# The first stage's transpose of normalized x: TensorE, or memory and VectorE

## The reference, cut to what matters

```python
mod = (_silu(L0_c) @ L0_wmod).reshape(L0_c.shape[0], 6, 1, -1)
sa, ca, ga, sb, cb, gb = (mod[:, n] for n in range(6))
ga = (2 * (ga >= 0) - 1) * jnp.maximum(jnp.abs(ga), 0.25)     # gb alike
h = _layernorm(x) * (1 + ca) + sa
x = x + ga * attention(h, wq, wk, wv, wo)          # 32 query heads, 8 key/value heads of 32
h = _layernorm(x) * (1 + cb) + sb
x = x + gb * experts(h, router, A, B)              # top 2 of 4 low-rank experts
```

## Time and profile before

| | us |
|---|---|
| median of 3 runs | 2801.24 (2797.73 to 2801.27) |
| the profiled execution | 2795.91 |
| its span | 2794.1 |
| PE busy | 2752.4 |
| DVE busy | 2181.9 |
| ACT busy | 1529.4 |
| POOL busy | 1909.4 |

### The profile page before, as it was taken

How to read it: one execution, slowest core, us unless ns; L and a number is a source line. 1 busy time by engine, 2 the same in 40 slices (tenths; PEclk the granted TensorE clock), 3 DMA queues, 4 the chain that set the end, 5 groups by cost and what they waited for, 6 DMA issues and landing times.

```text
span 2794.1 us, 48987 instructions
## 1 busy us (share of the span) xinstructions
PE 2752.4 (99%) x14654; PEld 1695.8 (61%) x14654; DVE 2181.9 (78%) x2809; ACT 1529.4 (55%) x2959; POOL 1909.4 (68%) x710
## 2 busy tenths in 40 slices
PE   7999999999999999999999999999999999999998
PEld 4788888884444444444444444444444447888887
DVE  4433434348999999999999999999999968676667
ACT  3211111116777676777767777767777764455454
POOL 2433333317999999999999999999999996111110
PEclk9999999999999999999999999999999999999999
DMA  7544443434444334334334334344444443323332
GB/s 268 181 144 137 147 139 132 137 116 137 91 88 100 87 87 100 85 87 100 85 87 100 85 89 98 89 90 93 93 90 91 97 123 114 113 96 108 113 100 81
DMA packets 167645, 307.05 MB, mean 110 GB/s; under 512 B 50001, under 2 KB 91409, under 8 KB 159505
## 3 DMA queue, kind: packets, MB, share of 16 engines
q1 hardware_dynamic: 158496, 240.05, 29.5%
q0 software_dynamic: 9072, 66.06, 11.6%
HBM read 159.12 MB, written 79.82 MB: 86 GB/s over the span
## 4 chain that ended last, share of the span: by engine, by line
PE 74%; DVE 2%; ACT 0%; issue 0%; DVEq 0%; POOL 0%; ACTq 0%; POOLq 0%
PE back_ps L1348 22%; PE back_ps L1362 18%; PE s_ps L1322 17%; PE s_ps L1938 11%; PE back_ps L1379 2%; PE back_ps L1987 2%; PE back_ps L2006 1%; PE back_ps L1959 1%; DVE mx L1237 1%; PE back_ps L1337 0%; PE s_ps L1411 0%; DVE a_lo L1281 0%; ACT h_t L1719 0%; DVE two_sum L1252 0%; DVE xn L1793 0%
## 5 line engine op out<-in xcount | busy, mean ns | idle before, releaser
L1218 ACT ACTIVATE p_t<-back_ps 128x512 f32<-128x512 f32 x2048 | 1114.7, 596 | 432.5 <-PE back_ps L1348 390.7
L1237 DVE TENSOR_REDUCE mx<-s_ps 128x1 f32<-128x1024 f32 x1002 | 1172.4, 1208 | 83.9 <-PE s_ps L1322 76.2
L1128 POOL TENSOR_TENSOR p_sum<-p_sum,p_t 128x2048 f32<-128x2048 f32 x254 | 1166.2, 4591 | 24.8 <-ACT p_t L1218 7.9
L1348 PE MATMUL back_ps<-q_st,k_st 98*128 98x512 f32 x2048 | 809.9, 436 | 3.4 <-POOL ones L1097 2.4
L1348 PEld LDWEIGHTS back_ps<-q_st,k_st 98*128 98x128 f32 x2048 | 343.9, 187 | 592.1 <-ACT p_t L1218 495.7
L1322 PE MATMUL s_ps<-k_st,q_st 96*128 96x512 f32 x2004 | 633.0, 397 | 0.6 <-DVE mx L1237 0.3
L1362 PE MATMUL back_ps<-p_t,v_sb 128*32 128x512 f32 x4096 | 545.8, 605 | 0.0
L1322 PEld LDWEIGHTS s_ps<-k_st,q_st 96*128 96x128 f32 x2004 | 379.0, 189 | 72.5 <-DVE mx L1237 3.2
L574 POOL TENSOR_TENSOR o_lo<-side,o_hi 128x512 fp32r<-128x512 f32 x80 | 104.2, 1303 | 321.4 <-ACT o_hi L544 321.2
L1252 DVE TENSOR_REDUCE two_sum<-p_t 128x512 f32<-128x1024 f32 x256 | 317.8, 1243 | 2.1 <-ACT p_t L1218 2.1
L1128 POOL TENSOR_TENSOR p_sum<-p_t 128x2048 f32<-128x2048 f32 x64 | 312.9, 4889 | 8.6 <-ACT p_t L1218 8.6
(11 more groups left out here) (186 smaller groups left out, 2910.8 us busy)
## 6 DMA issues: line engine op xcount, KB each, us to landing
p_sum<-two_sum POOLq DMA_DIRECT2D x63, 1024.0 KB, 6.9
q_st<-q_hi_d SPq DMA_DIRECT2D x128, 256.0 KB, 4.3
stage<-w_mod SPq DMA_DIRECT2D x48, 512.0 KB, 6.4
q_hi_d<-o_hi SPq DMA_DIRECT2D x64, 256.0 KB, 2.0
q_lo_d<-o_lo SPq DMA_DIRECT2D x64, 256.0 KB, 2.0
...
att_d<-a_sb SPq DMA_DIRECT2D x128, 128.0 KB, 2.3
...
```

Of the source, the lines that this page charges most:

```text
L1128: nc.gpsimd.tensor_tensor(total, before, p_t[:, kt, :, :], ALU.add).then_inc(sum_done, 1)
L1218: nc.scalar.activation(p_t[:, s, c, :], st_ps[:, c % 2, :], ACT.Exp, scale=SCALE)\
L1237: nc.vector.tensor_reduce(mx[:, slot % 2, e:e + 1], s_ps[:, e % 2, :], AX_X, ALU.max)\
L1348: nc.tensor.matmul(st_ps[:, c % 2, :], k_st[:, slot // 2, s * P:(s + 1) * P], q_st[:, slot, jj, h * QW:(h + 1) * QW], start=True, stop=True)\
```

## The change

In blocks 1 to 7 the normalized x of a half is no longer turned by PE. "away" stores the half to a new internal tensor `xn_d` (1 MB, one DMA, rows of 4 KB). "back" loads it with four DMAs, one for each quarter of the partitions, in runs of 32 numbers (128 bytes), into `squares`, which is the space of slots 2 and 3 of `stage`: for each tile of 128 features the squares of 32 x 32 then lie where a transpose within the square completes the whole transpose. DVE does that, one instruction of 128 x 256 a tile, into the same PSUM tile as before, and its scale-and-shift follows with a wait for it. Block 0's own h still goes through PE. "rows" has two slots left, so it comes in four parts of two slots where it came in two parts of four. The tables of events move stats, norm and turn of both halves.

```diff
...
@@ -215,23 +218,27 @@
 
 
 
-    PREPARE = {-1: [("fetch", 0)], 0: [("stats", 0)], 1: [("norm", 0)], 2: [("turn", 0, 0), ("turn", 0, 1)],
-               3: [("turn", 0, 2), ("turn", 0, 3)], 4: [("turn", 0, 4), ("turn", 0, 5)],
-               5: [("turn", 0, 6), ("turn", 0, 7), ("fetch", 1)], 7: [("stats", 1)], 8: [("norm", 1)],
-               9: [("turn", 1, 0), ("turn", 1, 1)], 10: [("turn", 1, 2), ("turn", 1, 3)],
+
+    PREPARE = {-1: [("fetch", 0)], 0: [("stats", 0), ("norm", 0)], 1: [("away", 0)], 2: [("back", 0), ("fetch", 1)],
+               4: [("stats", 1), ("norm", 1), ("turn", 0, 0), ("turn", 0, 1), ("turn", 0, 2)],
+               5: [("turn", 0, 3), ("turn", 0, 4), ("turn", 0, 5), ("away", 1)], 6: [("turn", 0, 6), ("turn", 0, 7)],
+               7: [("back", 1)], 9: [("turn", 1, 0), ("turn", 1, 1)], 10: [("turn", 1, 2), ("turn", 1, 3)],
                11: [("turn", 1, 4), ("turn", 1, 5)], 12: [("turn", 1, 6), ("turn", 1, 7)]}
 
-    MODULATE = {-1: [("rows", 0)], 3: [("mod", 0), ("rows", 1)], 11: [("mod", 1)]}
-
-
-    PREPARE_FIRST = {-1: [("fetch", 0)], 3: [("stats", 0)], 4: [("norm", 0)],
-                     5: [("turn", 0, 0), ("turn", 0, 1), ("turn", 0, 2)],
-                     6: [("turn", 0, 3), ("turn", 0, 4), ("turn", 0, 5)],
-                     7: [("turn", 0, 6), ("turn", 0, 7), ("fetch", 1)], 8: [("stats", 1)], 9: [("norm", 1)],
-                     10: [("turn", 1, 0), ("turn", 1, 1), ("turn", 1, 2)],
-                     11: [("turn", 1, 3), ("turn", 1, 4), ("turn", 1, 5)],
-                     12: [("turn", 1, 6), ("turn", 1, 7)]}
-    MODULATE_FIRST = {6: [("rows", 0)], 8: [("mod", 0), ("rows", 1)], 11: [("mod", 1)]}
+    MODULATE = {-1: [("rows", 0)], 2: [("mod", 0), ("rows", 1)], 5: [("mod", 1), ("rows", 2)],
+                8: [("mod", 2), ("rows", 3)], 11: [("mod", 3)]}
+
+
+    PREPARE_FIRST = {-1: [("fetch", 0)], 2: [("stats", 0), ("norm", 0)], 3: [("away", 0)], 4: [("fetch", 1)],
+                     5: [("back", 0)],
+                     6: [("stats", 1), ("norm", 1)], 7: [("turn", 0, 0), ("turn", 0, 1), ("turn", 0, 2), ("away", 1)],
+                     8: [("turn", 0, 3), ("turn", 0, 4), ("turn", 0, 5), ("turn", 0, 6), ("turn", 0, 7)],
+                     9: [("back", 1)],
+                     11: [("turn", 1, 0), ("turn", 1, 1), ("turn", 1, 2)],
+                     12: [("turn", 1, 3), ("turn", 1, 4), ("turn", 1, 5)],
+                     13: [("turn", 1, 6), ("turn", 1, 7)]}
+    MODULATE_FIRST = {5: [("rows", 0)], 7: [("mod", 0), ("rows", 1)], 9: [("mod", 1), ("rows", 2)],
+                      11: [("mod", 2), ("rows", 3)], 13: [("mod", 3)]}
 
 
     BESIDE_LAST = {-1: [("pairs",)], 12: [("negate",)], 13: [("scores", AHEAD - 2), ("scores", AHEAD - 1)]}
...
@@ -314,6 +321,7 @@
         h_lo = (sb("h_lo0", [P, KT, BLK], F32R), sb("h_lo1", [P, KT, BLK], F32R))
         stage = at("stage", [P, SLOTS, D], F32, q_at)
         xn = at("xn", [P, HT, D], F32, q_at + SLOTS * D * 4)
+        squares = stage[:, MOD_SLOTS:SLOTS, :].rearrange("p s (k n) -> p (s k) n", n=HALF)
         h_f = sb("h_f", [P, 2, HALF], F32)
         side = sb("side", [P, 3 * BLK + 4 * HALF], F32)
         o_hi = at("o_hi", [P, 2, BLK], F32R, q_at + (SLOTS + HT) * D * 4)
...
@@ -383,10 +394,30 @@
             def _(sp):
                 def fetch(half):
 
-                    if not is_int(half, 0):
-                        sp.wait_ge(turned, half * KT)
+                    if is_int(half, 2):
+                        sp.wait_ge(turned, 2 * KT)
+                    elif not is_int(half, 0):
+                        sp.wait_ge(xn_out, half * 16 - 32)
                     sp.dma_start(xn[:, :, :], x[bass.ds(half * HALF, HALF), :].rearrange("(t p) d -> p t d", p=P))\
                       .then_inc(x_in, 16)
+
+                def put_away(half):
+                    sp.wait_ge(xn_ready, half + 1)
+                    sp.dma_start(xn_d[bass.ds(half * HALF, HALF), :].rearrange("(t p) d -> p t d", p=P), xn[:, :, :])\
+                      .then_inc(xn_out, 16)
+
+                def bring_back(half):
+
+
+
+                    if is_int(half, 2):
+                        sp.wait_ge(wkv_lo_done, KT)
+                    for n in range(4):
+                        src = xn_d[bass.ds(half * HALF, HALF), :].rearrange("(b t) (k n c) -> n t k b c", t=32, n=4, c=32)[n]
+                        dst = squares[32 * n:32 * n + 32, :, :].rearrange("t k (b c) -> t k b c", c=32)
+                        if n == 0:
+                            sp.wait_ge(xn_out, half * 16 - 16)
+                        sp.dma_start(dst, src).then_inc(squares_in, 16)
 
                 sp.dma_start(cs[:, :, :], c_t).then_inc(small_in, 16)
                 sp.dma_start(ident[:, :], ident_in).then_inc(small_in, 16)
...
@@ -481,12 +516,12 @@
 
                                 sp.wait_ge(wkv_lo_done, KT)
 
-                            sp.wait_ge(stage_used, vec * (2 * SLOTS) + (MOD_CHUNKS + ev[1] * SLOTS))
-                            for s in range(SLOTS):
+                            sp.wait_ge(stage_used, vec * KT + (MOD_CHUNKS + ev[1] * MOD_SLOTS))
+                            for s in range(MOD_SLOTS):
                                 sp.dma_start(stage[:, s, :],
-                                             w_mod_t[:, ev[1] * SLOTS + s, bass.ds(vec * D + 2 * D, D)])\
+                                             w_mod_t[:, ev[1] * MOD_SLOTS + s, bass.ds(vec * D + 2 * D, D)])\
                                   .then_inc(stage_in[s], 16)
-                        elif ev == ("mod", 1):
+                        elif ev == ("mod", MOD_PARTS - 1):
                             sp.wait_ge(row_ready, vec + 1)
                             for j in range(4):
                                 src = slice(32 * j, 32 * j + 25, 8)
...
@@ -645,13 +680,20 @@
                             hf, kt = ev[1:]
                             tile = tile_at(i, hf, kt)
                             bank = bank_at(i, hf, kt)
-                            dve.wait_ge(turned, tile + 1)
+                            source = t_ps[:, bank, 0:HALF]
+                            if is_int(i, -1):
+                                dve.wait_ge(turned, tile + 1)
+                            else:
+                                if kt == 0:
+                                    dve.wait_ge(squares_in, i * 128 + 64 * hf + 64)
+                                nc.vector.transpose(source, squares[:, kt, :]).then_inc(x_turned_done, 1)
+                                dve.wait_ge(x_turned_done, tile - 2 * KT + 1)
                             if not (is_int(i, -1) and kt == 0):
 
                                 dve.wait_ge(h_lo_done, tile - 1)
 
                             at = b + par
-                            nc.vector.tensor_scalar(h_f[:, bank, :], t_ps[:, bank, 0:HALF],
+                            nc.vector.tensor_scalar(h_f[:, bank, :], source,
                                                     scale1[:, kt, bass.ds(at, 1)], shift[:, kt, bass.ds(at, 1)],
                                                     ALU.mult, ALU.add).then_inc(h_ready, 1)
                         elif ev[0] == "group":
...
@@ -732,7 +774,9 @@
 
                 def do(i, b, par, evs, vec):
                     for ev in evs:
-                        if ev[0] == "turn":
+                        if ev[0] == "turn" and not is_int(i, -1):
+                            pass
+                        elif ev[0] == "turn":
                             hf, kt = ev[1:]
                             half = i * 2 + (2 + hf)
                             tile = tile_at(i, hf, kt)
```

More of the change, by code:

```diff
@@ L105, in adaln_block @@
     att_d = nc.dram_tensor("att_d", (NIT, P, S), F32, kind="Internal").ap()
+    xn_d = nc.dram_tensor("xn_d", (NTOK, D), F32, kind="Internal").ap()
     mod_raw_d = nc.dram_tensor("mod_raw_d", (4, NB, D), F32, kind="Internal").ap()
@@ L135, in adaln_block @@
         project(nc, x, w_q, w_k, w_v, b_q, b_k, b_v, c_t, w_mod, ident_in, ident,
-                q_hi_d, q_lo_d, k_hi_d, k_lo_d, v_d, mod_raw_d, mod_gate_d, ahead, q_at, k_at, m_at)
+                q_hi_d, q_lo_d, k_hi_d, k_lo_d, v_d, xn_d, mod_raw_d, mod_gate_d, ahead, q_at, k_at, m_at)
         wo_hi = keep("wo_hi", [P, KT, D], F32R)
@@ L193, in project @@
 def project(nc, x, w_q, w_k, w_v, b_q, b_k, b_v, c_t, w_mod, ident_in, ident,
-            q_hi_d, q_lo_d, k_hi_d, k_lo_d, v_d, mod_raw_d, mod_gate_d, ahead, q_at, k_at, m_at):
+            q_hi_d, q_lo_d, k_hi_d, k_lo_d, v_d, xn_d, mod_raw_d, mod_gate_d, ahead, q_at, k_at, m_at):
     NTOK, D = x.shape
@@ L210, in project @@
     SLOTS = 4
+    MOD_SLOTS = 2
+    MOD_PARTS = KT // MOD_SLOTS
     MOD_CHUNKS = 2 * KT
@@ L360, in project @@
         turned = sem("turned")
+        xn_out = sem("xn_out")
+        squares_in = sem("squares_in")
+        x_turned_done = sem("x_turned_done")
         h_ready = sem("h_ready")
@@ L439, in do @@
```

(16 more changed lines are left out.)

## The result

The changed kernel takes 2844.1 us (median of 4 runs, 2841.7 to 2845.4) against 2800.2 of the kernel before beside it (4 runs, 2797.7 to 2801.3): ratio 1.0161, 95% interval 1.0146 to 1.0176 (the two medians alone give 1.0157). It is slower by 43.9 us. The profiled execution took 2841.73 us, its span 2839.9. Times are medians of an experiment's executions, where one execution of e6 (5252.6 us) and one of e7 (6592.1 us), in a far slower state, are left out.

The account below looks back on a forecast made before the run. PE bounds the loop before; afterwards the chain through one queue makes it wait. Block 0 14.8, block 1 7, blocks 3 and 5 2 x 4.0, even blocks 3 x 3.4: 40 us on 2801.2 gives 2841, range 2815 to 2870.

Parts of the forecast that it names:

- S: Queue time of a half's squares: 6.6 us from the v store's row, plus 1.6 of start and landing.
- lower bound of 3.5: Lowest S considered, in us: squares loading as fast as the fetch's full rows; total then 2798.
- odd block's chain: Odd loop blocks: fetch, stats, norm, store, squares, tiles for both halves take 73.7 us against 69.7, +4.0.
- Even blocks: Blocks 2, 4, 6: gate weight loads ahead of the second squares and DVE's clipping give 77.5 against 74.1, +3.4 each.
- Block 0: Block 0: gate-weight waits of 12.7 and 9.8 us and last tiles' 3.8 give 74.8 against 60.0, +14.8.
- the wait at the end: Block 0's end: the last tiles, coming late, add 3.8 us.
- Block 1: Block 1: an odd block whose fetch waits longer behind late gate stores, +7 us.
- What PE no longer does: Blocks 0 to 6: 112 tiles of 0.245 us leave PE, 27.4 us; block 0's 4.5 of air mostly goes too.
- The slope: Whole sum: seven blocks hold S twice each, so the added time is 40 + 14 (S - 6.6) us.
- The transpose: DVE's transpose of 128 x 256: 0.43 us taken, between 0.35 and 0.69.
- rival of the fast squares: Squares come fast, so removed PE work is gain: 2798 us with S at 3.5, about 2788 possible; chance 0.24.
- a doubling on top of the row: Skill's below-512 B rule applied to the v store's row: S at 13, total at the upper bound, 2935 us.

Follow-up runs that it names:

- e6: The kernel before with only the gate's weights loaded in four parts instead of two, PE still turning x; 2807.0 us, ratio 1.0026.
- e7: The changed kernel with block 0's turning on PE, fetch ahead of squares, stores right behind norm, last tiles one event earlier; 2796.6 us, ratio 0.9991.
- e11: The changed kernel with only three of a half's four loads of squares (part of h wrong); 2827.6 us, ratio 1.0106.
- e1: The changed kernel with the squares loaded in runs of 8 KB instead of 128 bytes (h wrong); 2818.2 us, ratio 1.0073.
- e3: The changed kernel with 26 unread matmuls added in PE's wait ahead of blocks 2, 4 and 6; 2837.7 us, ratio 1.0142.
- e8: The kernel before without PE's 112 tiles of transposes for blocks 1 to 7, nothing in their place (h wrong); 2786.1 us, ratio 0.9949.
- e5: The changed kernel with block 0 preparing block 1 by PE's transposes as before the change; 2824.7 us, ratio 1.009.
- e10: The changed kernel with only the gate's small stores moved to event 5 of the following odd block; 2846.5 us, ratio 1.0164.
- e2: The changed kernel with 224 PE transposes of a constant put back at their old places, result unread; 2847.9 us, ratio 1.0182.
- e9: e7 with the gate's eight small stores moved to event 5 of the following odd block; 2783.3 us, ratio 0.9945.
- e4: The changed kernel with the second half's fetch issued before the first half's squares in blocks 1 to 6; 2827.6 us, ratio 1.0105.

## Why the prediction was right, step by step

The forecast was 2841 and the measured time 2844.1, with the sign and the mechanism right. In the stretch of the table I had 40 us and it was 40.5, but that is luck in good part: block 0 came out 4.1 over its term, block 1 4.1 and blocks 3 and 5 together 1.7, and the even blocks 9.4 under theirs.

- **S.** Right. 8.2 us from issue to landing were forecast (1.6 + 6.6) for a half's squares, from the v store's row; 8.1, 8.2 and 8.8 stand in blocks 3, 5 and 1, and e11's quarter took off 1.7. The lower bound of 3.5 was out of reach: in e1, with rows of 8 KB, S is 5.1 to 5.4 by the same reckoning. My steps let the second fetch stand behind the squares on the DMA engines; what holds it is the issue of the four loads, 5.1 to 5.8 us of SP's list, which no row had shown.
- **The odd block's chain.** Right to about a microsecond until the squares. From PE's start of block 3 (296.3) to after's rows: stats 9.4 (7.9 forecast), away 17.7 (17.3), back 21.9 (22.7), second stats 34.4 (34.5), away 46.2 (47.2), back 53.3 (53.9), squares 61.4 (62.5; the steps as written add up to 62.1). PE waits 6.0, not 8.1. With the norm at 1.5 us for two tiles instead of 2.5 and the store landing in 4.2 instead of 5.4, the chain is shorter than I made it. (POOL works for 1.3 us beside the norm in before and not at all in after; whether that is the cause no run tests.) The block still grew by 4.2 and 5.4 (4.0 forecast).
- **The clock.** Missed; no term of the sum has it. In e3 it is worth 6.4 us in the loop. In block 0 PE is busy for 3.88 and 5.48 us at about 0.50 (the windows), half of which, 4.7, would be saved; so some 11 in all, as between after and e8. It made good what the shorter chain gave back.
- **Even blocks.** Wrong: +3.4 each forecast, +0.5, +0.5 and -0.1 measured. I let them wait for the second squares. They do not wait: store and norm are quicker than in my steps, and the gate's two parts are PE's work meanwhile. e11 shows it. What PE gained there by the change, from 74.0 us busy to 71.4, went into waits of 2.4 to 3.2 us a block for the gate's weights and for the last tiles.
- **Block 0.** +18.9 instead of +14.8, and e5 shows that the round trip is the cause. The two waits for the gate's weights are 9.6 and 8.3 (12.7 and 9.8 forecast), less than I had, and so is the wait at the end, 3.1 (3.8). But two shorter waits for the weights (1.3 and 0.7) and the 4.7 of the clock come to them.
- **Block 1.** +11.1 instead of +7. The reason was forecast, late gate stores ahead of the fetch; e6 has 5.2 us by them without any square, though taking them away gave back only 2.9 in e10.
- **What PE no longer does.** 27.4 us and 4.5 of air forecast; 22.7 in all in e8, of which block 0 has 3.4. In the changed kernel they are worth 3.8 to 5.5 (e2).
- **The slope.** "Seven blocks hold S twice each" gave 14 us for each us of S, and e11's 22.0 for 1.65 is 13.3. The agreement is luck: the even blocks do not hold S, and the odd ones fell by twice what it gives them.
- **The transpose.** 0.43 forecast, 0.45 measured:

```profile
L689 DVE STREAM_TRANSPOSE s_ps<-stage x112: 447/450/460, 93.4 to 591.4; 128x256 f32<-128x256 f32 x112
```

The rival of the fast squares fell with S. Yet its floor was near: it put 2788 where every loop block is PE's own. e9 reaches 2783 with the squares as slow as they are, by another order of the queue and with block 0's turning back on PE. What I had taken for a property of S was in good part a property of the order: I should have asked what the chain costs with the fetch ahead of the squares (e4), since a fetch that needs nothing but the store stands there for 5 us behind loads that it does not need.

The rule of the Trainium skill on short transfers ("DMA: Bandwidth & Descriptors", "Specifications"), read as a doubling on top of the row, would have put S at 13. The runs show 6.5 and so decide against that reading; against rows of 8 KB the short runs are 1.2 to 1.4 times as slow (6.5 to 7.2 against 5.1 to 5.4).
